# Widening a row of counts from SBUF, half by a transfer and half by GpSimd copies

## What is computed

```python
edge_index = jnp.stack([src, dst])
h = jnp.maximum(_layernorm(x, axis=-1), 0.0)
x = x + _L0_gnn_ref(h, edge_index, ...)
...
def _L0_gnn_ref(x, edge_index, W1, ...):
    h = x
    for i in range(3):
        agg = jax.ops.segment_sum(h[src], dst, num_segments=6250)
        h = h + agg
        h = jnp.maximum(_bn(h @ W1[i] + b1[i], ...), 0.0)
        h = jnp.maximum(_bn(h @ W2[i] + b2[i], ...), 0.0)
    return h
```

## Time and profile before

| | |
|---|---|
| median of 3 runs | 4138.2 us (4132.59 to 4138.64) |
| the profiled execution, its own time | 4137.52 us |
| its span in the trace | 4135.9 us |
| TensorE busy | 3774.8 us (91%) |
| VectorE busy | 3061.5 us (74%) |
| ScalarE busy | 2479.4 us (60%) |
| GpSimd busy | 1381.2 us (33%) |
| granted TensorE clock, mean | 0.99 |

### The profile page before, as it was taken

The page is one execution under the profiler, slowest core; times in us unless marked ns, Lnnn a source line. Parts: engine busy times, 40 slices in busy tenths (PEclk is TensorE's granted clock), DMA queues, the critical chain, the costliest instruction groups (busy, mean ns, idle before and its releaser), DMA issues.

```text
span 4135.9 us, 59814 instructions
## 1 busy us (share of the span) xinstructions
PE 3774.8 (91%) x17331; PEld 2948.2 (71%) x17331; DVE 3061.5 (74%) x5526; ACT 2479.4 (60%) x4705; POOL 1381.2 (33%) x2017
## 2 busy tenths in 40 slices
PE   0128889999999999999899999999999999999999
PEld 0116578888888644555588888888888888887887
DVE  9989956577677677887668767766866876786685
ACT  1118756656656787787565655565565565566655
POOL 0021135533545320000362343244244234456624
PEclk9999999999999999999899999999999999999999
DMA  2019964544543322222143344344444334433444
GB/s 63 0 52 381 364 224 125 141 130 124 144 128 107 95 69 76 70 66 56 46 114 107 107 130 120 108 125 122 111 120 122 110 104 130 119 97 108 114 133 135
DMA packets 234209, 496.24 MB, mean 120 GB/s; under 512 B 32579, under 2 KB 100924, under 8 KB 227223
## 3 DMA queue, kind: packets, MB, share of 16 engines
q1 hardware_dynamic: 213084, 432.93, 36.6%
q0 software_dynamic: 7856, 53.36, 3.6%
q10 hardware_dynamic: 12938, 6.05, 0.7%
HBM read 409.83 MB, written 43.87 MB: 110 GB/s over the span
## 4 chain that ended last, share of the span: by engine, by line
PE 50%; issue 0%; DVE 0%; POOL 0%; ACT 0%; ACTq 0%; POOLq 0%; DVEq 0%
PE ps L2170 40%; PE ps L2288 3%; PE ps L2289 3%; PE ps L2291 1%; PE ps L2290 1%; PE ps L2332 1%; PE ps L2313 0%; PE ps L2318 0%; PE ps L2274 0%; PE ps L2202 0%; PE ps L2208 0%; PE ps L2193 0%; ACT wide L2017 0%; PE ps L2185 0%; POOL inv L2072 0%
## 5 line engine op out<-in xcount | busy, mean ns | idle before, releaser
L2170 PE MATMUL ps<-wide,hi 128*128 128x512 f32 (+2 forms) x5537 | 2139.0, 389 | 26.2 <-issue 11.0
L2170 PE MATMUL ps<-wide,lo 128*128 128x512 f32 (+2 forms) x5537 | 2078.2, 379 | 0.0
L2017 DVE CAST wide<-ring 128x1536 fp32r<-128x1536 uint8 (+2 forms) x1274 | 1311.1, 1029 | 560.8 <-PE ps L2170 555.1
L2170 PEld LDWEIGHTS ps<-wide,hi 128*128 128x128 f32 x5537 | 1043.0, 188 | 230.8 <-issue 32.9
L2170 PEld LDWEIGHTS ps<-wide,lo 128*128 128x128 f32 x5537 | 1044.8, 189 | 186.1
L2017 ACT CAST wide<-ring 128x768 fp32r<-128x768 uint8 (+1 forms) x1274 | 1153.1, 905 | 4.3 <-DMA ring<-count 3.0
L2384 ACT CAST hi<-high 128x128 fp32r<-128x128 f32 x1274 | 381.6, 300 | 991.5 <-PE ps L2170 616.2
L2109 POOL TENSOR_TENSOR lo<-hN,high 128x128 fp32r<-128x128 f32 x686 | 567.7, 831 | 757.9 <-PE ps L2170 469.2
L2109 POOL TENSOR_TENSOR lo<-hB,high 128x128 fp32r<-128x128 f32 x588 | 497.5, 847 | 763.3 <-PE ps L2170 543.9
L2166 PE MATMUL ps<-hN,hB 128*128 128x512 f32 (+1 forms) x1274 | 525.3, 569 | 5.6 <-DVE aggT L2347 4.2
L2377 ACT ACTIVATE hN<-aggT,source_scores 128x512 f32<-128x512 f32 (+1 forms) x637 | 428.8, 695 | 118.1 <-PE ps L2166 86.9
(11 more groups left out here) (247 smaller groups left out, 3498.5 us busy)
## 6 DMA issues: line engine op xcount, KB each, us to landing
ring<-count SPq DMA_DIRECT2D x490, 320.0 KB, 2.9
ring<-count SPq DMA_DIRECT2D x441, 256.0 KB, 2.6
ring<-count SPq DMA_DIRECT2D x490, 224.0 KB, 2.5
wide<-count POOLq DMA_DIRECT2D x49, 1024.0 KB, 5.7
count<-aggT SPq DMA_DIRECT2D x49, 800.0 KB, 5.1
xN<-in_x ACTq DMA_DIRECT2D x1, 2744.0 KB
out<-xN SPq DMA_DIRECT2D x1, 1064.0 KB
out<-xN SPq DMA_DIRECT2D x1, 896.0 KB
```

Source lines behind the costliest of these rows:

```text
L2017: return copy(wide[:, g % WIDE_SLOTS, c0:c1].rearrange("p (t u f) -> p t u f", u=2, f=P), rows[:, g % row_slots, c0:c1].rearrange("p (t f ...
L2170: ins = e.matmul(ps[:, c, 0:size], part[:, g % CUT_SLOTS, :], wide[:, g % WIDE_SLOTS, w0:w0 + size], start=k == 0 and part is hi, stop=k = ...
```

## The change

`fill_counts` no longer reads the row back from DRAM. The 2048 bytes of the early third are widened straight from the row buffer: the last 1024 by a transfer that GpSimd issues as soon as three of the row's four groups are evacuated, the first 1024 by a GpSimd copy. From the third block on the copy waits until `lo` of the block two before is made, so it starts when VectorE has come to the end of a period. There are three row buffers instead of two; the third lies in the early third's own columns of `aggT`, and the last additions wait until it is free. The lag of the sums is three blocks instead of four. ScalarE, before it fills a buffer again, also waits for the copy and the transfer that read it. TensorE waits for the copy at the first piece and for the transfer at the third. SyncE waits for all stores at the end, since nobody else does.

```diff
-EARLY_LAG = 4
+EARLY_LAG = 3
+EARLY_COPIED = 2
+ROW_BUFFERS = 3
...
-        rows = [net.aggT[:, c0:c0 + ROW // 4].bitcast(U16) for c0 in (0, early.stop)]
+        rows = [net.aggT[:, c0:c0 + ROW // 4].bitcast(U16) for c0 in (0, early.start, early.stop)]
...
             e.wait_ge(s["state"], NB)
+            e.wait_ge(stored[1], 16 * len(range(1, NB, ROW_BUFFERS)))
+            e.wait_ge(s["copied"], NB)
...
                             e.wait_ge(s["lo"], j + 1)
+                            e.wait_ge(s["copied"], j + 1)
+                        if g == EARLY_COPIED:
                             e.wait_ge(s[f"loaded{j % EARLY_SLOTS}"], j // EARLY_SLOTS * 16 + 16)
...
-                if k >= 2:
-                    e.wait_ge(stored[k % 2], 16 * (k // 2))
+                if k >= ROW_BUFFERS:
+                    j = k - ROW_BUFFERS
+                    e.wait_ge(stored[k % ROW_BUFFERS], 16 * (k // ROW_BUFFERS))
+                    e.wait_ge(s["copied"], j + 1)
+                    e.wait_ge(s[f"loaded{j % EARLY_SLOTS}"], j // EARLY_SLOTS * 16 + 16)
...
         @block.gpsimd
         def _(e):
-            t0 = THIRD_PAIRS[EARLY][0]
+            c0 = THIRD_PAIRS[EARLY][0] * PAIR
+            c1, c2 = c0 + pieces[EARLY_COPIED][0], c0 + width
+            near, far = ((c - 1) // (PER * PAIR) + 1 for c in (c1, c2))
             for k in range(NB):
-                e.wait_ge(stored[k % 2], 16 * (k // 2 + 1))
+                row = rows[k % ROW_BUFFERS].bitcast(U8)
                 if k >= EARLY_SLOTS:
                     e.wait_ge(s["summed"], k - EARLY_SLOTS + 1)
-                e.dma_start(wide[:, k % EARLY_SLOTS, :], count[k * P:(k + 1) * P, t0 * PAIR:t0 * PAIR + width])\
-                    .then_inc(s[f"loaded{k % EARLY_SLOTS}"], 16)
+                e.wait_ge(s["out"], groups * k + max(near, far))
+                e.dma_start(wide[:, k % EARLY_SLOTS, c1 - c0:width], row[:, c1:c2]).then_inc(s[f"loaded{k % EARLY_SLOTS}"], 16)
+                if 1 < k < NB - 1:
+
+                    e.wait_ge(s["lo"], k - 1)
+                e.tensor_copy(wide[:, k % EARLY_SLOTS, 0:c1 - c0], row[:, c0:c1]).then_inc(s["copied"], 1)
...
+            for u in range(ROW_BUFFERS):
+                e.wait_ge(stored[u], 16 * len(range(u, NB, ROW_BUFFERS)))
```

More of the change, by code:

```diff
@@ L543, in fill_counts @@
     assert len(pieces) == groups == 4
-    names = ["left", "apart", "right", "mm", "out", "spread", "normal", "turned", "state", "high", "hi", "lo", "summed", "whole",
+    names = ["left", "apart", "right", "mm", "out", "spread", "normal", "turned", "state", "high", "hi", "lo", "summed", "whole", "copied",
              *[f"loaded{j}" for j in range(EARLY_SLOTS)]]
@@ L554, in fill_counts @@
         early = slice(THIRDS[EARLY][0] * P, sum(THIRDS[EARLY]) * P)
-        rows = [net.aggT[:, c0:c0 + ROW // 4].bitcast(U16) for c0 in (0, early.stop)]
+        rows = [net.aggT[:, c0:c0 + ROW // 4].bitcast(U16) for c0 in (0, early.start, early.stop)]
+        assert len(rows) == len(stored) == ROW_BUFFERS
         codes_by = net.aggT[:, ROW // 4:ROW // 4 + CODE_SLOTS * codes_each // 2].bitcast(I16)
-        assert early.start >= ROW // 4 + CODE_SLOTS * codes_each // 2 and early.stop + ROW // 4 <= NP and early.stop - early.start == width
+        assert early.start >= ROW // 4 + CODE_SLOTS * codes_each // 2 and early.stop + ROW // 4 <= NP and early.stop - early.start == width >= ROW // 4
         def of_block(table, k, run):
@@ L666, in _ @@
                     e.wait_ge(s["mm"], groups * k + g + 1)
-                    e.activation(rows[k % 2][:, t0 * P:t1 * P], ps[:, bank:bank + 2, :].rearrange("p b f -> p (b f)")
+                    e.activation(rows[k % ROW_BUFFERS][:, t0 * P:t1 * P], ps[:, bank:bank + 2, :].rearrange("p b f -> p (b f)")
                                  [:, 0:(t1 - t0) * P], ACT.Copy, scale=-1.0).then_inc(s["out"], 1)
@@ L691, in _ @@
                 e.wait_ge(s["out"], groups * (k + 1))
-                e.dma_start(count[k * P:(k + 1) * P, :], rows[k % 2].bitcast(U8)).then_inc(stored[k % 2], 16)
+                e.dma_start(count[k * P:(k + 1) * P, :], rows[k % ROW_BUFFERS].bitcast(U8)).then_inc(stored[k % ROW_BUFFERS], 16)
+            for u in range(ROW_BUFFERS):
+                e.wait_ge(stored[u], 16 * len(range(u, NB, ROW_BUFFERS)))
 def count_anything(nc, net, src, dst, count, more):
@@ L2745, in factor_work @@
             norm_rows(ch)
-        stored = [nc.alloc_semaphore(f"count_stored{u}_{nc.next_id()}") for u in (0, 1)]
+        stored = [nc.alloc_semaphore(f"count_stored{u}_{nc.next_id()}") for u in range(ROW_BUFFERS)]
         roots = [(bn[:, 0, :], vec[:, 4, :]), (rows_bn[:, 6, :], rows_bn[:, 4, :])]
```

## The result

The changed kernel took **4164.36 us** in the median of 7 runs (4162.63 to 4165.32); the kernel before, run beside it on the same chip, 4138.64. The ratio is **1.0058, 95% interval 1.0045 to 1.0070**: slower by 24 us by the ratio, by 25.7 us between the two medians. One of the seven executions of the kernel before took 7913.71 us, which a median does not follow. The profiled execution of the changed kernel took 4164.39 us, with a span of 4162.7; before it was 4137.5 and 4135.9. So 26.8 us are to be found between the two traces.

A forecast was written before the change was run, and what follows sets the result against it. The prediction took VectorE, at 4.78 us a block, to bound the fill, with the DMA queues just above at 4.98. From 4137.5 us, -9.4 (stalls) -9.5 (tail) +42 (copies) = +23 gave 4161 us, range 4115 to 4190.

The forecast's parts named there:

- (a): Fill loop: a 512 KB transfer from SBUF and three row buffers remove all transfer stalls, gaining 9.4 us.
- (b): Fill's tail, last `right` to last addition: a lag of three makes it 11.1 us instead of 20.6, gaining 9.5.
- (c): Fill: GpSimd copies and two-input VectorE operations hold each other off; 47 copies at 0.89 us cost VectorE 42 us.
- the DMA engines' 4.98 us a block: Fill: two queues' shares, 2.88 and 2.10 us a block, taken as a second limit just above VectorE's 4.78.
- the lower bound: Price of a GpSimd copy from below: 0.825 ns an element from a GpSimd fill, 0.84 us for 1024.
- the 0.05 for a handover: Added to each copy's 0.84 us for the change between VectorE and GpSimd, making 0.89 us a block.
- upper bound: Price of a GpSimd copy from above: two-input subtraction's 0.268 / 127 = 2.11 ns an element, 2.16 us a copy.
- (d): Fill loop: the period becomes 4.78 + 0.89 = 5.67 us, and no other engine is late.
- No hold-off for 16 bits: Rival: copies are free beside VectorE's 16-bit operations in the fill, so the kernel ends at 4119 us; chance 0.19.
- A dear copy: Rival: widening bytes takes over 1.5 us a copy from VectorE in the fill, 4207 us in the middle; chance 0.15.
- The matmul clock: Rival: idling TensorE stays at 1.2 GHz in the fill and sets the period, near 4285 us; chance 0.02.
- Partly held: Rival: VectorE loses only 0.2 to 0.6 us of each copy in the fill, 4128 to 4148 us; chance 0.04.

The follow-up runs named there:

- e5: Changed kernel with no GpSimd copy, the transfer widening all 2048 bytes; three buffers and lag of three stay: 4126.95 us, 0.9975 of the kernel before.
- e1: Changed kernel with the GpSimd copies left out from the fifth block on, half transfers kept: 4120.58 us, 0.9979 of the kernel before.
- e3: Changed kernel with a GpSimd zero fill, which reads nothing, replacing the copy from the fifth block on: 4121.0 us, 0.9983 of the kernel before.
- e4: Changed kernel with the copy waiting for `left` instead of `lo`, so it starts beside `right`: 4156.57 us, 1.0068 of the kernel before.
- e6: Changed kernel with ScalarE copying 512 bytes a row instead of GpSimd's copy, three quarters transferred: 4127.05 us, 0.9975 of the kernel before.
- after_again: Changed kernel unaltered, run again on the chip of e5 and e6: 4162.14 us, 1.0061 of the kernel before.

## Why the prediction was right

The forecast was 4161 us, slower; measured were 4164.4, within the range. By its own steps, against the two spans:

| step | forecast | measured | from |
|---|---|---|---|
| (a) transfer stalls | -9.4 | -9.4 | 238.8 - 229.4; no wait of ScalarE for a store is left, and the loop holds 48 x 4.78 and the copies only |
| (b) tail, last `right` to last addition | -9.5 | -9.6 | 20.6 to 11.0 |
| (c) 47 copies | +42 | +39.4 | 268.0 - 229.4 = 38.6 in the loop, 0.8 in the last `left` |
| outside the fill | 0 | +6.4 | start of the fill +6.2, the rest +0.2 |
| sum | +23 | +26.8 | |

(a) was right for this pair of executions. That the parts of its mechanism (third buffer, no round trip) remove the stalls without a halved transfer is shown by e5, though not which part. Its size is less firm than the prediction made it, 2.8 us in the other look at the kernel before. A part of its reasoning was not needed: the DMA engines' 4.98 us a block did not have to fall to 3.54. In e5 they stay full and the period is VectorE's. The last section shows that those shares are no measure of what the engines need.

(b) came out to 0.1 us of its 11.1. The transfer landed in 4.4 us, inside the 0 to 5.7 that were allowed, and was waited for once, 0.5 us at the last block. The slow period helped: with periods of 4.78 us TensorE waited 2.1 us (e1) and 1.7 us (e3) for the last block's half transfer, and the tail was 13.7 and 12.6 us.

That (a) and (b) agree to 0.1 us says that what the change removed is what the first trace held. Against the other trace of the kernel before the same steps would be worth 2.8 and 6.1 us.

(c) is the step that decided, and it held in each particular: the copy's record of 2.57 us holds its wait for `apart`, it ends inside `left`, `left` is longer by 0.84, and 16-bit operands make no exception. The price was put at 0.89 and measured at 0.84. The rate of GpSimd's IOTA, 0.825 ns an element, taken as the lower bound, was already the copy's rate (0.82); the 0.05 for a handover was not there, which makes most of the 2.6 us of the difference. (Its upper bound divides by 127 where 128x128 and 128x2 differ by 126 elements: 2.13 ns instead of 2.11, which changes nothing.) The prediction said only what two-input operations do. e4 shows that a one-input one on 16-bit data does the same, so there was no better place beside `right`.

(d) 5.62 us against 5.67, and nothing else late: TensorE idles 1.45 us a period and ScalarE waits for TensorE.

The rivals. *No hold-off for 16 bits* would have been 4119; e3, which has it in effect, took 4121. The two times do not start from the same kernel before, though. The forecast started from 4137.5, and beside e3 it took 4129.2: e3 gained 8.2 us, not 18.9, and the four copies that it keeps (its 48 periods took 232.5 us, not 229.4) account for 3.1 of the difference. So the nearness to 4119 is partly luck, and the rival's mechanism is out. *A dear copy* is out: 0.84 us and not over 1.5. *The matmul clock* is out: the fill's granted clock was 0.98 of 2.4 GHz, above the 0.94 before, although TensorE was busy for less of the fill. *Partly held* is out for copies that meet a running operation: each of the 44 periods of 5.62 us holds the whole 0.84.

So the small distance from the forecast, 3.4 us, is two errors against each other: the copies 2.6 us cheaper than put, and 6.4 us outside the fill that belong to no step. That the time came within 3.4 us is luck in part; the direction and the step that decides it are not, since the medians differ by 25.7 us here and by 26.3 beside e5 and e6 (4162.14 against 4135.8), and e1 takes the loss away with the copies.

## What to carry to other kernels

In these kernels a GpSimd copy that reads SBUF was not hidden beside a VectorE that works without a pause from SBUF. Count its streaming time as VectorE's, whichever instruction it is made to wait for, and ask a busy-share table which engine can take it instead (here ScalarE, or the transfer as it was). A GpSimd instruction that only writes SBUF was free at the same place. And test the parts of a bundle alone: the third row buffer, the transfer out of SBUF and the shorter lag were together worth 0.25%, and the copy that came with them cost more than three times that (4162.14 against 4126.95 us on the same chip).

## What the runs showed that was not expected

**A read that is passed over.** In most periods the waiting copy got in at the first change of instruction on VectorE. Not always: in e1_no_copy the third copy, issued as elsewhere 0.14 us after `apart` began, got in nowhere for three blocks. GpSimd of that kernel:

```profile
310.82 15.17 POOL L703 CAST wide<-aggT 128x1024 fp32r<-128x1024 uint8 x1 [0.28 <-DVE lo L599]
```

and VectorE, in which `apart`, `left`, `right`, `high` and `lo` follow each other without a pause up to here:

```profile
331.10 1.83 DVE L582 TENSOR_TENSOR apart<-marks_by,aggT 128x3200 int16<-128x3200 int16 x1 [6.01 <-PE ps L626]
```

The copy ended at 310.82 + 15.17 = 325.99 us, 0.90 us after VectorE had run out of work (331.10 - 6.01 = 325.09), since TensorE, waiting for the copy, gave no buffers back; VectorE then stood idle for 6.01 us. In after_again another third copy took 5.62 us instead of 2.57. It began at 316.62, passed `apart`, `left`, `right`, `high` and `lo`, and ended at 322.24, again 0.90 us after VectorE had run out of work, for 0.17 us this time (321.34). So both got in only at a pause of VectorE; being second in line gave no turn before that. What decides between the first boundary and none stays open: the starts look alike in the trace, 0.14 us after `apart` as in the regular periods.

**Full queues that slow nobody.** In e5 the two queues took 57.7% and 42.3% of the DMA engines' time, together all of it, for 230 us, with landings of 6.5 us for the 1024 KB. VectorE lost nothing by it. In e6, with a quarter fewer bytes in the load, the same view has:

```profile
q1 hardware_dynamic: 6766, 38.50, 56.2%
q0 software_dynamic: 6749, 36.95, 43.2%
```

The stores are the same 38.5 MB, and their share went from 42.3% to 56.2% when the other queue's fell. Together the two fill the time again, with 75 MB instead of 88. So a share in this view is not the time that the bytes need, and adding the two to 4.98 us a block, as the prediction did, or to 4.3, as the expectation of e6 did, finds no limit. Here the waits decide: in e5 and e6 the loop has one period of 4.9 to 5.0 us and otherwise VectorE's own.
